# Causal attention on one core: every pair's first head keeps its probabilities whole in fp32, the second is always split

## The chip, the cores and the metric

One core of one Trainium2 chip runs the whole program. The metric is the device time of one execution in microseconds. Before the change it was run three times.

## The reference, cut to what matters

The input x is 4 images of 64 channels and 32 x 32 = 1024 places. Three layers follow each other; the one that the change touches most is the second.

```python
# layer 1, on x as (b, 64, 1024): media attention, one head, no mask
att = softmax(einsum('bmi,bmj->bij', k, q), axis=2)
x = x + einsum('cm,bmn->bcn', wo, einsum('bij,bmj->bmi', att, v))
# layer 2, on tokens t = (b, 1024, 64): causal attention, 8 heads of 64
q, k, v = (layernorm(t) @ W for W in (Wq, Wk, Wv))          # (b, 8, 1024, 64)
scores = where(causal, -1e30, einsum('bhqd,bhkd->bhqk', q, k) / 8)
t = t + (softmax(scores) @ v).reshape(b, 1024, 512) @ Wo
# layer 3: recurrence over the 1024 tokens, batch-normalised input
y[t] = sigmoid(wx[t] + y[t-1] @ V.T);  t = t + y
```

## The kernel before, in words

**Items.** The attention scores are made transposed, keys on the 128 partitions and 512 queries (four tiles of 128) along a PSUM bank. One such bank is an item. The first layer has 16 items in each of 4 units (one unit a batch), slots 0 to 63. The causal layer has 16 units, each two heads of one batch (a pair, `r` = 0 and 1), with 9 items a head: 36 tiles of the lower triangle, packed four to an item by `ATTN_RUNS`. Items of the two heads alternate, so item n of a unit belongs to head n % 2, and one slot of two items is worked at a time: `g`, `g+1`. There are 64 + 288 items.

**What happens to an item.** TensorE makes the scores of both heads in three fp16 products (keys high x queries high and low, keys low x queries high; `pe_scores`, L526, matmul at L537), after identity products that add the mask where a tile is on the diagonal (L522). ScalarE takes the exponential to fp32 (`act_item`, L775, to the tile `probs`) and, for a split item, once more to fp16 (L779, `probs_high`). GpSimd subtracts the second from the first into `probs_low` (`pool_low`, L1250). Three slots later (`LAG` = 6 items) TensorE multiplies by the values, the probabilities being the stationary side, a tile at a time (`pe_values`, L545): three fp16 products for a split item (L574 high x values high, L576 high x values low, L578 low x values high), or one fp32 product for a whole item (L570, `probs` x `values`). The column of ones behind the 64 values gives the denominator. VectorE divides (`dve_scale`, L975) and GpSimd adds the result to the tokens (L1260).

**Which items are whole.** `whole(i)` (L143) decides it for all engines: in the first layer every 4th item, in the causal layer the last of every 6, so n = 5, 11 and 17 of a unit of 18, all of head 1.

**Buffers and waits.** Scores have three banks (`ST_RING`): TensorE waits until ScalarE is through with the item two before (L517). `probs` and the fp16 parts are rings of ten items. Before ScalarE overwrites a place of `probs` it waits for GpSimd's low part of the item ten before, or, if that one was whole, for TensorE's values of it (L770 to L773). The third item of each head (`SPLIT_ITEM`) has half its tiles' values done a slot later (`value_runs`, L126).

**What lies beside it.** Each slot also makes, for the unit after the next, the products whose row maxima are subtracted (`pe_maxes`, L497, masks at L483), and VectorE reduces them (L903); they have two banks, each freed by VectorE. Auxiliary steps share one more bank: queries (two a unit), values (two a unit, four token tiles each for both heads), the maxima transposed (L614), keys (L651). The products of these steps go through `pe_split_product` (L455, L456). For values, ScalarE copies the bank to `values` in fp32 and to `values_high` in fp16 (L810, L811), and VectorE subtracts to `values_low` (L959). GpSimd also works on the layer norms of each batch (`pool_ln1`, `pool_newton`, L1269 to L1296) between its low parts.

The order on TensorE in a slot is: values of the items six before, auxiliary steps, masks of the maxima, masks of the scores, maxima, scores. Every engine runs its own list in this order of slots, without reordering. After the last item the third layer follows (from L698).

Of the kernel before, what the change touches and what calls it, by code (L numbers as in the profile page):

```python
# [26 lines left out]
ST_RING, P_RING, E_RING, Q_RING, S_RING = 3, 10, 10, 3, 4  # L27
LAG = 6

CONV_WHOLE, ATTN_WHOLE = 4, 6  # L30
LN_EPS = 1e-5


# [79 lines left out]
def unit_of(i):  # L113
    return i // CONV_ITEMS if i < CONV_ITEMS * B else B + (i - CONV_ITEMS * B) // (2 * ATTN_ITEMS)
# [28 lines left out]
def whole(i):  # L143

    n = i - first_slot(unit_of(i))
    period = CONV_WHOLE if unit_of(i) < B else ATTN_WHOLE
    return n % period == period - 1


def rests(i):  # L150
# [77 lines left out]
def build(nc, x_cm, x_tm, conv_w, conv_vo, attn_w, ffn, gb, const, out):  # L228
# [5 lines left out]
    with ctx:  # L234
# [37 lines left out]
        e32 = sb("probs", [P, E_RING, CW])  # L272
        p_hi = sb("probs_high", [P, P_RING, CW], f16)
        p_lo = sb("probs_low", [P, P_RING, CW], f16)
        v32 = [sb(f"values{i}", [P, NT, 2, PO]) for i in range(2)]
        v_hi = [sb(f"values_high{i}", [P, NT, 2, PO], f16) for i in range(2)]
        v_lo = [sb(f"values_low{i}", [P, NT, 2, C], f16) for i in range(2)]
        scaled = sb("scaled_outputs", [P, S_RING, TPC, C])
        rden = sb("reciprocal_denominators", [P, S_RING, TPC])
        cmx = [sb(f"conv_partial_max{i}", [P, NT, NC]) for i in range(2)]  # L280
# [264 lines left out]
        def pe_values(i):  # L545
            v = unit_of(i)
            n = i - first_slot(v)
            r = 0 if v < B else n % 2
            if n == 0:
                nc.tensor.wait_ge(s_aux_used, values_ready(v))  # L550
            if whole(i):
                nc.tensor.wait_ge(s_probs, i + 1)
            else:
                nc.tensor.wait_ge(s_rest, rests(i))
            for item, (j, t0, tiles, at) in value_runs(i):
                for k in range(tiles):
                    c, t = (t0 + k) // TPC, (t0 + k) % TPC
                    half = half_of(v, c, r)
                    opens = half not in OPENED
                    if opens:  # L560
                        OPENED.add(half)
                        if half == B * NC + 1:
                            pe_wait_bank(OUTPUT_BANK_HAD)
                        elif 1 <= half <= B * NC:
                            nc.tensor.wait_ge(s_scaled, half)
                        elif half:
                            nc.tensor.wait_ge(s_scaled, half - 1)
                    cols, dst = slice((at + k) * P, (at + k + 1) * P), output_bank(half)[:, t * PO:t * PO + PO]
                    if whole(item):
                        ins = nc.tensor.matmul(dst, e32[:, item % E_RING, cols], v32[v % 2][:, j, r, :],  # L570
                                               start=opens, stop=True, skip_group_check=True)
                        continue
                    hi, lo = p_hi[:, item % P_RING, cols], p_lo[:, item % P_RING, cols]
                    nc.tensor.matmul(dst, hi, v_hi[v % 2][:, j, r, :], start=opens, stop=False,  # L574
                                     skip_group_check=True)
                    nc.tensor.matmul(dst[:, 0:C], hi, v_lo[v % 2][:, j, r, :], start=False, stop=False,  # L576
                                     skip_group_check=True)
                    ins = nc.tensor.matmul(dst, lo, v_hi[v % 2][:, j, r, :], start=False, stop=True,  # L578
                                           skip_group_check=True)
            ins.then_inc(s_values, 1)  # L580

# [207 lines left out]
        def act_aux(m):  # L789
            _, _, what, k = AUXES[m]  # L790
            bank = aux_bank(m)
            if what in ("max_transpose", "max_transpose_half"):
                return
            nc.scalar.wait_ge(s_aux, m + 1)
            if what == "conv_matrix":
                nc.scalar.activation(wov_hi[:], bank[:, 0:C], ACT.Copy).then_inc(s_aux_cast, 1)
            elif what == "project":
                act_project(bank, k).then_inc(s_aux_cast, 1)
            elif what == "conv_values":

                if k >= 2:
                    nc.scalar.wait_ge(s_values, first_slot(k - 1))
                x = bank[:].rearrange("p (t c) -> p t c", c=C)
                nc.scalar.activation(v32[k % 2][:, :, 0, 0:C], x, ACT.Copy)
                nc.scalar.activation(v_hi[k % 2][:, :, 0, 0:C], x, ACT.Copy).then_inc(s_aux_cast, 1)
            elif what == "values":
                v, c = k // 2, k % 2
                nc.scalar.wait_ge(s_values, first_slot(v - 1))
                x, tiles = bank[:].rearrange("p (t r c) -> p t r c", r=2, c=C), slice(c * TPC, (c + 1) * TPC)
                nc.scalar.activation(v32[v % 2][:, tiles, :, 0:C], x, ACT.Copy)  # L810
                nc.scalar.activation(v_hi[v % 2][:, tiles, :, 0:C], x, ACT.Copy).then_inc(s_aux_cast, 1)  # L811
            elif what == "queries":
                nc.scalar.activation(q_hi[k // 2 % Q_RING][:, k % 2 * CW:(k % 2 + 1) * CW], bank[:],
                                     ACT.Copy).then_inc(s_aux_cast, 1)
            elif what == "matrix":
                nc.scalar.activation(of_heads(a_hi if k < 2 else pr_hi, k % 2), by_pair(bank),
                                     ACT.Copy).then_inc(s_aux_cast, 1)
            elif what == "keys":
                nc.scalar.activation(xs_hi[:, k * CW:(k + 1) * CW], bank[:], ACT.Copy).then_inc(s_aux_cast, 1)
            elif what == "ln3_transpose":  # L820
                nc.scalar.activation(xh3T[:, k * CW:(k + 1) * CW], bank[:], ACT.Copy).then_inc(s_aux_used, 1)
            else:
                nc.scalar.activation(wx_raw[:, k * CW:(k + 1) * CW], bank[:], ACT.Copy).then_inc(s_aux_used, 1)
# [117 lines left out]
        def dve_aux(m):  # L941
# [4 lines left out]
            if what == "conv_matrix":  # L946
                nc.vector.tensor_tensor(out=wov_lo[:], in0=bank[:, 0:C], in1=wov_hi[:],
                                        op=ALU.subtract).then_inc(s_aux_used, 1)
            elif what == "project":
                dve_project(bank, k).then_inc(s_aux_used, 1)  # L950
            elif what == "matrix":
                hi, lo = (of_heads(x, k % 2) for x in ((a_hi, a_lo) if k < 2 else (pr_hi, pr_lo)))
                nc.vector.tensor_tensor(out=lo, in0=by_pair(bank), in1=hi, op=ALU.subtract).then_inc(s_aux_used, 1)
            elif what == "conv_values":
                nc.vector.tensor_tensor(out=v_lo[k % 2][:, :, 0, :], in0=bank[:].rearrange("p (t c) -> p t c", c=C),
                                        in1=v_hi[k % 2][:, :, 0, 0:C], op=ALU.subtract).then_inc(s_aux_used, 1)
            elif what == "values":
                v, tiles = k // 2, slice(k % 2 * TPC, (k % 2 + 1) * TPC)
                nc.vector.tensor_tensor(out=v_lo[v % 2][:, tiles, :, :],  # L959
                                        in0=bank[:].rearrange("p (t r c) -> p t r c", r=2, c=C),  # L960
                                        in1=v_hi[v % 2][:, tiles, :, 0:C], op=ALU.subtract).then_inc(s_aux_used, 1)
            elif what == "queries":
                v, cols = k // 2, slice(k % 2 * CW, (k % 2 + 1) * CW)
                nc.vector.tensor_tensor(out=q_lo[v % Q_RING][:, cols], in0=bank[:], in1=q_hi[v % Q_RING][:, cols],
                                        op=ALU.subtract).then_inc(s_aux_used, 1)
            elif what == "keys":
                cols = slice(k * CW, (k + 1) * CW)
                nc.vector.tensor_tensor(out=xs_lo[:, cols], in0=bank[:], in1=xs_hi[:, cols],
                                        op=ALU.subtract).then_inc(s_aux_used, 1)
            elif what == "wx":  # L970
                nc.vector.wait_ge(s_aux_used, m + 1)
                for h in range(2):
                    nc.vector.bn_stats(bst[:, 2 * k + h, :], wx_raw[:, (2 * k + h) * HW:(2 * k + h + 1) * HW])
# [106 lines left out]
        def _(dve):  # L1080
# [10 lines left out]
                                        op=ALU.subtract).then_inc(s_x16, 1)  # L1091
            for i in range(2):
                nc.vector.memset(amx[i][:], -3e38)
                nc.vector.memset(v32[i][:, :, :, C:PO], 1.0)
                nc.vector.memset(v_hi[i][:, :, :, C:PO], 1.0)
                ins = nc.vector.memset(y16[i][:, :, 0:1], 0.0)
            ins.then_inc(s_init, 1)
            for k in range(3):
# [377 lines left out]
```

## Time and profile before

| what | us |
|---|---|
| median of three runs | 568.92 |
| lowest, highest run | 566.38, 571.42 |
| profiled execution (the page gives its span, and no time beside it) | 567.0 |
| TensorE matmuls busy in it | 490.0 (86%) |
| ScalarE / GpSimd / VectorE busy | 429.3 / 424.4 / 398.8 |
| causal items: first scores, last values | about 110.9, 519.6 |

How to read it: PE is TensorE's matmul side and PEld its weight loads, which run ahead of and under the matmuls; DVE is VectorE, ACT ScalarE, POOL GpSimd, SP SyncE. Times of rows are from the start of the span. Matmuls are pipelined, so that the duration of one (some 196 ns for 65 columns) is no measure of how many fit in a microsecond; the distance from one weight load to the next is.

### The profile page before, as it was taken

How to read it: one execution, taken by the hardware profiler on the slowest of the kernel's cores; microseconds unless marked ns; L12 is line 12 of the kernel's file. 1: busy time of each engine (PE TensorE's matmuls, PEld its weight loads, DVE VectorE, ACT ScalarE, POOL GpSimd, SP SyncE). 2: the span in 40 equal slices, each digit the busy share in tenths (PEclk: the TensorE clock that was granted, in tenths of full speed). 3: DMA queues.
4: the chain of work that ended last, by engine and by line, in shares of the span. 5: the costliest groups of instructions: out<-in, count | busy, mean ns of one | idle time of the engine just before them, and what ended most of it. 6: DMA issues, size and time to landing. Idle time of an engine off the chain costs nothing.

```text
span 567.0 us, 16744 instructions
## 1 busy us (share of the span) xinstructions
PE 490.0 (86%) x6771; PEld 323.0 (57%) x6771; DVE 398.8 (70%) x909; ACT 429.3 (76%) x832; POOL 424.4 (75%) x463
## 2 busy tenths in 40 slices
PE   4699978988799998889999988998999999787783
PEld 1277655655565755565666756565666766564431
DVE  5878888767678786576767676766767786328757
ACT  3488867866778878587888878787888878785593
POOL 3867965857988797968788797899788799985002
PEclk9999999989999999799999999999999999998698
DMA  9100000000000000000000000000000000000001
GB/s 230 68 3 2 2 20 1 4 1 3 1 22 2 3 3 2 3 1 21 2 3 2 4 3 1 21 3 1 1 3 3 2 3 2 2 2 2 0 2 74
DMA packets 3580, 7.46 MB, mean 13 GB/s; under 512 B 1168, under 2 KB 1456, under 8 KB 3376
## 3 DMA queue, kind: packets, MB, share of 16 engines
q1 hardware_dynamic: 3056, 5.34, 3.5%
q8 instruction: 54, 0.88, 0.7%
q10 hardware_dynamic: 448, 1.05, 0.6%
q14 instruction: 22, 0.18, 0.1%
HBM read 4.22 MB, written 1.05 MB: 9 GB/s over the span
## 4 chain that ended last, share of the span: by engine, by line
PE 45%; DVE 22%; POOL 17%; ACT 9%; issue 6%; DMA 1%; DVEq 0%; SPq 0%; POOLq 0%; ACTq 0%
POOL probs_low L1250 10%; PE bank L537 9%; DVE attn_partial_max L903 7%; ACT probs_high L779 6%; PE bank L497 6%; PE bank L570 5%; PE bank L574 4%; DVE conv_partial_max L897 3%; PE bank L578 3%; PE bank L576 3%; PE bank L455 2%; PE bank L522 2%; PE bank L483 2%; PE bank L456 2%; POOL tokens L1260 2%
## 5 line engine op out<-in xcount | busy, mean ns | idle before, releaser
L1250 POOL TENSOR_TENSOR probs_low<-probs,probs_high 128x512 f16<-128x512 f32 x288 | 327.6, 1158 | 77.5 <-ACT probs_high L779 76.7
L775 ACT ACTIVATE probs<-bank 128x512 f32<-128x512 f32 x352 | 214.7, 611 | 84.2 <-PE bank L537 69.0
L903 DVE TENSOR_REDUCE attn_partial_max<-bank 128x1 f32<-128x512 f32 (+2 forms) x288 | 185.3, 685 | 99.5 <-PE bank L497 99.0
L779 ACT ACTIVATE probs_high<-bank 128x512 f16<-128x512 f32 x288 | 176.8, 614 | 0.0
L574 PEld LDWEIGHTS bank<-values_high,probs_high 128*128 128x128 f16 x1152 | 105.7, 98 | 74.2 <-issue 35.8
L574 PE MATMUL bank<-values_high,probs_high 128*128 128x65 f16 x1152 | 128.8, 196 | 15.5 <-POOL probs_low L1250 11.4
L576 PE MATMUL bank<-values_low,probs_high 128*128 128x64 f16 x1152 | 127.6, 194 | 0.0
L578 PE MATMUL bank<-values_high,probs_low 128*128 128x65 f16 x1152 | 127.1, 194 | 0.0
L576 PEld LDWEIGHTS bank<-values_low,probs_high 128*128 128x128 f16 x1152 | 106.9, 99 | 3.2
L578 PEld LDWEIGHTS bank<-values_high,probs_low 128*128 128x128 f16 x1152 | 107.2, 98 | 0.0
L570 PE MATMUL bank<-values,probs 128*128 128x65 f32 x512 | 71.7, 278 | 0.8 <-POOL probs_low L1250 0.8
L570 PEld LDWEIGHTS bank<-values,probs 128*128 128x128 f32 x512 | 64.7, 192 | 3.5 <-POOL probs_low L1250 1.0
L497 PE MATMUL bank<-attn_keys_high,queries_high 64*128 64x512 f16 (+3 forms) x384 | 56.7, 332 | 7.9 <-ACT probs_high L779 6.0
L1260 POOL TENSOR_TENSOR tokens<-scaled_outputs,tokens 128x256 f32<-128x256 f32 x71 | 51.7, 729 | 8.0 <-DVE scaled_outputs L983 3.3
L537 PE MATMUL bank<-queries_high,attn_keys_high 64*128 64x512 f16 (+3 forms) x384 | 55.6, 326 | 1.1 <-ACT probs_high L779 1.1
L537 PE MATMUL bank<-queries_high,attn_keys_low 64*128 64x512 f16 (+3 forms) x384 | 55.5, 325 | 0.0
L537 PE MATMUL bank<-queries_low,attn_keys_high 64*128 64x512 f16 (+3 forms) x384 | 55.5, 325 | 0.0
L897 DVE TENSOR_REDUCE conv_partial_max<-bank 128x1 f32<-128x512 f32 x64 | 42.8, 687 | 5.8 <-PE bank L470 4.7
L983 DVE TENSOR_TENSOR scaled_outputs<-bank,reciprocal_denominators 128x256 f32<-128x256 f32 x72 | 30.6, 425 | 7.6 <-DVE reciprocal_denominators L979 0.5
L522 PE MATMUL bank<-causal_masks,identity_bf 128*128 128x128 bf16 x256 | 27.5, 219 | 6.6 <-ACT probs_high L779 6.4
L497 PEld LDWEIGHTS bank<-attn_keys_high,queries_high 64*128 64x128 f16 x384 | 15.3, 93 | 29.7 <-issue 6.8
L1343 POOL TENSOR_TENSOR x_split<-probs 128x512 f32<-128x512 f32 x4 | 4.2, 1092 | 36.1 <-ACT probs L878 36.1
(192 smaller groups left out, 708.9 us busy)
## 6 DMA issues: line engine op xcount, KB each, us to landing
x_channels<-in_x_cm SPq DMA_DIRECT2D x6, 256.0 KB, 7.6
tokens<-in_x_tm SPq DMA_DIRECT2D x1, 1024.0 KB, 10.4
out<-ln_channels SPq DMA_DIRECT2D x4, 256.0 KB, 2.0
attn_weights<-in_attn_w ACTq DMA_DIRECT2D x1, 512.0 KB, 6.2
attn_keys_split<-attn_keys_high SPq DMA_DIRECT2D x4, 128.0 KB, 2.3
attn_keys_split<-attn_keys_low SPq DMA_DIRECT2D x4, 128.0 KB, 2.4
queries_high<-minus_max_rows SPq DMA_DIRECT2D x32, 2.0 KB
x_channels<-in_x_cm ACTq DMA_DIRECT2D x2, 128.0 KB, 3.2
```

Source lines behind the costliest of these rows:

```text
L497: last[r] = nc.tensor.matmul(prep_bank(m + r)[:, at * P:(at + tiles) * P], q[rows(r), t * P:(t + 1) * P], xs_hi[rows(r), b * N + j0 * P:b ...
L537: last[r] = nc.tensor.matmul(ST[(i + r) % ST_RING][:, at * P:(at + tiles) * P], keys[rows(r), b * N + j * P:b * N + (j + 1) * P], queries[ ...
L570: ins = nc.tensor.matmul(dst, e32[:, item % E_RING, cols], v32[v % 2][:, j, r, :], start=opens, stop=True, skip_group_check=True)
L574: nc.tensor.matmul(dst, hi, v_hi[v % 2][:, j, r, :], start=opens, stop=False, skip_group_check=True)
L576: nc.tensor.matmul(dst[:, 0:C], hi, v_lo[v % 2][:, j, r, :], start=False, stop=False, skip_group_check=True)
L578: ins = nc.tensor.matmul(dst, lo, v_hi[v % 2][:, j, r, :], start=False, stop=True, skip_group_check=True)
L775: ins = nc.scalar.activation(e32[:, i % E_RING, :], o[:], ACT.Exp, scale=scale)
L779: ins = nc.scalar.activation(p_hi[:, i % P_RING, :], o[:], ACT.Exp, scale=scale)
L897: nc.vector.reduce_max(cmx[v % 2][:, t, part:part + 1], o[:], AX).then_inc(s_prep_used, 1)
L903: nc.vector.reduce_max(dst, o[:].rearrange("p (n w) -> p n w", n=n), AX).then_inc(s_prep_used, 1)
L1250: nc.gpsimd.tensor_tensor(out=p_lo[:, i % P_RING, :], in0=e32[:, i % E_RING, :], in1=p_hi[:, i % P_RING, :], op=ALU.subtract).then_inc(s_r ...
L1260: nc.gpsimd.tensor_tensor(out=dst, in0=scaled[:, half % S_RING, :, :], in1=dst, op=ALU.add).then_inc(s_added, 1)
```

## The change

In the causal layer every item of head 0 of a pair (n even) is whole and every item of head 1 is split. The values of head 0 are then kept only in fp32 and those of head 1 only as fp16 high and low parts, so that each of ScalarE's two copies and VectorE's subtraction handles one head. The first layer keeps its rule of every fourth item. Its values move to buffers without the head dimension.

```diff
-CONV_WHOLE, ATTN_WHOLE = 4, 6
+CONV_WHOLE = 4
+WHOLE_HEAD, SPLIT_HEAD = 0, 1
...
 def whole(i):
     n = i - first_slot(unit_of(i))
-    period = CONV_WHOLE if unit_of(i) < B else ATTN_WHOLE
-    return n % period == period - 1
+    return n % CONV_WHOLE == CONV_WHOLE - 1 if unit_of(i) < B else n % 2 == WHOLE_HEAD
...
-        v32 = [sb(f"values{i}", [P, NT, 2, PO]) for i in range(2)]
-        v_hi = [sb(f"values_high{i}", [P, NT, 2, PO], f16) for i in range(2)]
-        v_lo = [sb(f"values_low{i}", [P, NT, 2, C], f16) for i in range(2)]
+        v32 = [sb(f"values{i}", [P, NT, PO]) for i in range(2)]
+        v_hi = [sb(f"values_high{i}", [P, NT, PO], f16) for i in range(2)]
+        v_lo = [sb(f"values_low{i}", [P, NT, C], f16) for i in range(2)]
...
-                        ins = nc.tensor.matmul(dst, e32[:, item % E_RING, cols], v32[v % 2][:, j, r, :],
+                        ins = nc.tensor.matmul(dst, e32[:, item % E_RING, cols], v32[v % 2][:, j, :],
...
-                nc.scalar.activation(v32[v % 2][:, tiles, :, 0:C], x, ACT.Copy)
-                nc.scalar.activation(v_hi[v % 2][:, tiles, :, 0:C], x, ACT.Copy).then_inc(s_aux_cast, 1)
+                nc.scalar.activation(v32[v % 2][:, tiles, 0:C], x[:, :, WHOLE_HEAD, :], ACT.Copy)
+                nc.scalar.activation(v_hi[v % 2][:, tiles, 0:C], x[:, :, SPLIT_HEAD, :], ACT.Copy).then_inc(s_aux_cast, 1)
...
-                nc.vector.tensor_tensor(out=v_lo[v % 2][:, tiles, :, :],
-                                        in0=bank[:].rearrange("p (t r c) -> p t r c", r=2, c=C),
-                                        in1=v_hi[v % 2][:, tiles, :, 0:C], op=ALU.subtract).then_inc(s_aux_used, 1)
+                nc.vector.tensor_tensor(out=v_lo[v % 2][:, tiles, :],
+                                        in0=bank[:].rearrange("p (t r c) -> p t r c", r=2, c=C)[:, :, SPLIT_HEAD, :],
+                                        in1=v_hi[v % 2][:, tiles, 0:C], op=ALU.subtract).then_inc(s_aux_used, 1)
```

The remaining lines of the diff drop the head index from the other value products (L574 to L578), from the first layer's copies (L804, L805, L955) and from the two memsets that write the columns of ones (L1094, L1095).

## Rows read from the trace of the kernel before

**Rows 1.** The page, part 1: busy time, share of the span, instructions.
```profile
PE 490.0 (86%) x6771; PEld 323.0 (57%) x6771; DVE 398.8 (70%) x909; ACT 429.3 (76%) x832; POOL 424.4 (75%) x463
```

**Rows 2.** Who waited for whom: engine, line, waited for, us in total, times, longest.
```profile
ACT probs L775 <- PE bank L537: 69.0, 105, 4.1
...
PEld bank L574 <- POOL probs_low L1250: 33.4, 56, 3.6
...
PE bank L574 <- POOL probs_low L1250: 11.4, 17, 3.1
```

**Rows 3.** The page, part 5: costliest groups, busy us and mean ns, idle before.
```profile
L1250 POOL TENSOR_TENSOR probs_low<-probs,probs_high 128x512 f16<-128x512 f32 x288 | 327.6, 1158 | 77.5 <-ACT probs_high L779 76.7
...
L779 ACT ACTIVATE probs_high<-bank 128x512 f16<-128x512 f32 x288 | 176.8, 614 | 0.0
L574 PEld LDWEIGHTS bank<-values_high,probs_high 128*128 128x128 f16 x1152 | 105.7, 98 | 74.2 <-issue 35.8
...
L570 PEld LDWEIGHTS bank<-values,probs 128*128 128x128 f32 x512 | 64.7, 192 | 3.5 <-POOL probs_low L1250 1.0
```

**Rows 4.** Timeline of PEld, 302 to 327: start us, us, what, [idle before].
```profile
302.34 0.10 PEld L574 LDWEIGHTS bank<-values_high,probs_high 128*128 128x128 f16 x1 [0.21 <-issue]
...
304.64 0.10 PEld L574 LDWEIGHTS bank<-values_high,probs_high 128*128 128x128 f16 x1 [0.42 <-issue]
...
305.36 0.10 PEld L455 LDWEIGHTS bank<-attn_keys_split,qk_matrix_high 128*128 128x128 f16 x1
...
306.93 0.10 PEld L574 LDWEIGHTS bank<-values_high,probs_high 128*128 128x128 f16 x1 [0.42 <-issue]
...
309.29 0.10 PEld L574 LDWEIGHTS bank<-values_high,probs_high 128*128 128x128 f16 x1 [0.42 <-issue]
...
312.00 0.10 PEld L574 LDWEIGHTS bank<-values_high,probs_high 128*128 128x128 f16 x1 [0.42 <-issue]
...
314.44 0.10 PEld L574 LDWEIGHTS bank<-values_high,probs_high 128*128 128x128 f16 x1 [0.42 <-POOL probs_low L1250]
...
317.69 0.10 PEld L574 LDWEIGHTS bank<-values_high,probs_high 128*128 128x128 f16 x1 [0.21 <-issue]
...
320.20 0.10 PEld L574 LDWEIGHTS bank<-values_high,probs_high 128*128 128x128 f16 x1 [0.42 <-POOL probs_low L1250]
...
322.91 0.10 PEld L574 LDWEIGHTS bank<-values_high,probs_high 128*128 128x128 f16 x1 [0.21 <-issue]
...
326.04 0.10 PEld L574 LDWEIGHTS bank<-values_high,probs_high 128*128 128x128 f16 x1 [0.21 <-issue]
```

**Rows 5.** Timeline of PEld, the same unit: where it stood behind value products.
```profile
303.64 0.12 PEld L497 LDWEIGHTS bank<-attn_keys_high,queries_high 64*128 64x128 f16 x2 [0.52 <-DVE attn_partial_max L903]
...
307.78 0.13 PEld L483 LDWEIGHTS bank<-causal_masks,identity_bf 128*128 128x128 bf16 x2 [0.15 <-DVE attn_partial_max L903]
...
319.00 0.13 PEld L522 LDWEIGHTS bank<-causal_masks,identity_bf 128*128 128x128 bf16 x2 [0.52 <-DVE attn_partial_max L903]
```

**Rows 6.** Timeline of PEld, 111.9 to 113.2: a whole item, then a split one.
```profile
111.89 0.97 PEld L570 LDWEIGHTS bank<-values,probs 128*128 128x128 f32 x8 [0.42 <-issue]
112.72 0.15 PEld L574 LDWEIGHTS bank<-values_high,probs_high 128*128 128x128 f16 x1
...
113.17 0.10 PEld L455 LDWEIGHTS bank<-value_matrix_high,attn_keys_split 128*128 128x128 f16 x1
```

**Rows 7.** Timelines of POOL and PEld near 227; then engines' busy us, clock 228 to 230.
```profile
226.55 0.61 POOL L1291 COPY ln_out<-ln_out 128x512 f32<-128x512 f32 x1
...
228.33 0.10 PEld L574 LDWEIGHTS bank<-values_high,probs_high 128*128 128x128 f16 x1 [3.58 <-POOL probs_low L1250]
...
228.00:230.00 2.00, 1.39 (x23) 1.23 (x24) 0.00 (x0) 0.00 (x0) 2.00 (x3) 0.50 0.00 0
```

**Rows 8.** Timelines of POOL and DVE at the end of the causal layer.
```profile
511.37 6.73 POOL L1250 TENSOR_TENSOR probs_low<-probs,probs_high 128x512 f16<-128x512 f32 x6
...
520.17 0.17 DVE L979 RECIPROCAL reciprocal_denominators<-bank 128x4 f32<-128x4 f32 x1
```

More of the change, by code:

```diff
@@ L573, in pe_values @@
                     hi, lo = p_hi[:, item % P_RING, cols], p_lo[:, item % P_RING, cols]
-                    nc.tensor.matmul(dst, hi, v_hi[v % 2][:, j, r, :], start=opens, stop=False,
+                    nc.tensor.matmul(dst, hi, v_hi[v % 2][:, j, :], start=opens, stop=False,
                                      skip_group_check=True)
-                    nc.tensor.matmul(dst[:, 0:C], hi, v_lo[v % 2][:, j, r, :], start=False, stop=False,
+                    nc.tensor.matmul(dst[:, 0:C], hi, v_lo[v % 2][:, j, :], start=False, stop=False,
                                      skip_group_check=True)
-                    ins = nc.tensor.matmul(dst, lo, v_hi[v % 2][:, j, r, :], start=False, stop=True,
+                    ins = nc.tensor.matmul(dst, lo, v_hi[v % 2][:, j, :], start=False, stop=True,
                                            skip_group_check=True)
@@ L803, in act_aux @@
                 x = bank[:].rearrange("p (t c) -> p t c", c=C)
-                nc.scalar.activation(v32[k % 2][:, :, 0, 0:C], x, ACT.Copy)
-                nc.scalar.activation(v_hi[k % 2][:, :, 0, 0:C], x, ACT.Copy).then_inc(s_aux_cast, 1)
+                nc.scalar.activation(v32[k % 2][:, :, 0:C], x, ACT.Copy)
+                nc.scalar.activation(v_hi[k % 2][:, :, 0:C], x, ACT.Copy).then_inc(s_aux_cast, 1)
             elif what == "values":
@@ L954, in dve_aux @@
             elif what == "conv_values":
-                nc.vector.tensor_tensor(out=v_lo[k % 2][:, :, 0, :], in0=bank[:].rearrange("p (t c) -> p t c", c=C),
-                                        in1=v_hi[k % 2][:, :, 0, 0:C], op=ALU.subtract).then_inc(s_aux_used, 1)
+                nc.vector.tensor_tensor(out=v_lo[k % 2][:], in0=bank[:].rearrange("p (t c) -> p t c", c=C),
+                                        in1=v_hi[k % 2][:, :, 0:C], op=ALU.subtract).then_inc(s_aux_used, 1)
             elif what == "values":
                 v, tiles = k // 2, slice(k % 2 * TPC, (k % 2 + 1) * TPC)
-                nc.vector.tensor_tensor(out=v_lo[v % 2][:, tiles, :, :],
-                                        in0=bank[:].rearrange("p (t r c) -> p t r c", r=2, c=C),
-                                        in1=v_hi[v % 2][:, tiles, :, 0:C], op=ALU.subtract).then_inc(s_aux_used, 1)
+                nc.vector.tensor_tensor(out=v_lo[v % 2][:, tiles, :],
+                                        in0=bank[:].rearrange("p (t r c) -> p t r c", r=2, c=C)[:, :, SPLIT_HEAD, :],
+                                        in1=v_hi[v % 2][:, tiles, 0:C], op=ALU.subtract).then_inc(s_aux_used, 1)
             elif what == "queries":
@@ L1093, in _ @@
                 nc.vector.memset(amx[i][:], -3e38)
-                nc.vector.memset(v32[i][:, :, :, C:PO], 1.0)
-                nc.vector.memset(v_hi[i][:, :, :, C:PO], 1.0)
+                nc.vector.memset(v32[i][:, :, C:PO], 1.0)
+                nc.vector.memset(v_hi[i][:, :, C:PO], 1.0)
                 ins = nc.vector.memset(y16[i][:, :, 0:1], 0.0)
```

## The prediction, as it was made before the result

> **What bounds the kernel now.** I read the page first: in the span of 567.0 us TensorE's matmuls are busy 86%, its weight loads 57%, and ScalarE, GpSimd and VectorE 70 to 76% [rows 1]. No engine is full, so the waits come next: ScalarE waits 69.0 us for TensorE's scores, while TensorE's value products wait for GpSimd's low parts (11.4 us on the matmul side, 33.4 us as the weight loads see it) [rows 2]. Each engine waits for the next in a circle. The groups give the prices: a low part on GpSimd 1.16 us, an exponential on ScalarE 0.61 us, and a weight load of 98 ns in fp16 against 192 ns in fp32 [rows 3].
>
> Then the weight loads in order of time. One unit of attention (two heads) is nine slots, each with the values of one pair of items, the next maxima and the next scores. Slot starts k=0 to 8 lie at 302.34, 304.64, 306.93, 309.29, 312.00, 314.44, 317.69, 320.20 and 322.91, and the next unit at 326.04 [rows 4]: lengths 2.30, 2.29, 2.36, 2.71, 2.44, 3.25, 2.51, 2.71 and 3.13, together 23.70 us. A pair of split items takes 304.64 to 305.36, 0.72 us, though it is 24 matmuls [rows 4]. After such a pair TensorE often stands still: in k=0 it could go on at 303.06 (0.72 behind 302.34) and goes on at 303.64; k=6 likewise (318.41, 319.00) [rows 4, 5]. The row names VectorE's maxima, but what comes last there is ScalarE: both exponentials of the item two back must end before a score bank is free, the same 2.3 us in each such slot. So in regular slots two loops tie: ScalarE's (two exponentials of one item, then 1.0 us of maxima and scores on TensorE) and TensorE's own.
>
> **The change, part by part.** Per unit 9 of 18 items are whole where 3 were: 6 more in each of 16 units, 96 in all. The conv items stay as they are.
>
> GpSimd loses 96 x 1.16 = 111 us, ScalarE 96 x 0.61 = 59 us [rows 3]. Neither is a gain by itself: it is worth what TensorE now waits for them.
>
> TensorE pays. A whole item of 4 tiles followed by a split one stands at 111.89: fp32 loads start at 111.89, the fp16 ones at 112.72, and the next work at 113.17 [rows 6]. The pair costs 0.83 + 0.45 = 1.28 us, against 0.72 for two split items: 0.56 us more. In a unit, k = 0, 1, 4, 6, 7 go from split+split to whole+split (5 x 0.56); k = 2, 5, 8 hold one whole item already and only change the order; k = 3 (which takes two tiles over from k = 2) gets four more whole tiles for four split ones, 0.51. That is 3.31 us a unit, 53 us over 16 units. All of it is on TensorE.
>
> Here the Trainium skill can be weighed. It says that a true fp32 product goes through the array in four passes ("FP8 and Floating Point Precision", TensorE Precision Notes). The three fp16 products of a tile (0.72/8 = 0.09 us) would then become 0.12 us; the trace has 0.83/4 = 0.21, so it disagrees with passes alone, and by passes the whole change would add only 12 us. The skill also says that the fast weight load is off for fp32 ("TensorE: Matmul & The Clock Gate", Weight-path perf modes); the trace's 192 against 98 ns agrees, and this is the rule that speaks against the change.
>
> What comes back is TensorE's standing time. With the first item whole, its bank is free after one exponential: 0.61 us plus some 0.15 us of hand-over, covered by 1.28 us of value products. So the stalls go: 0.55 us at k=0, 0.05 at k=1, 0.46 at k=2 (it continues at 307.78 and waits again before the maxima), 0.14 at k=3, 0.58 at k=6, 0.11 at k=8 [rows 4, 5], 1.89 us a unit; each is the gap between what the slot's pieces take where nothing holds them and what they take here. The regular unit becomes 23.70 + 3.31 - 1.89 = 25.1 us, now TensorE from end to end. Is another engine late next? ScalarE needs at most 3 x 0.61 = 1.83 us a slot and GpSimd one low part of 1.16 us with a few additions of outputs a unit [rows 3]; the slots average 2.79 us. The tightest is k=2, with values of two tiles each: I put it at 1.90 us, so ScalarE just fits there. If it didn't fit I would lose at most the 0.46 us, 7 us over all units.
>
> Fourteen units have the maxima beside them: 14 x 1.89 = 26.5 us. In the last two GpSimd is behind the whole time (six low parts in a row from 511.37, and VectorE's closing scale only at 520.17 [rows 8]); slot by slot I count 5.0 and 5.1 us back, 10.1 together, 1.2 of it behind the last scores, where 3 x 1.28 us of products remain.
>
> The other stalls behind GpSimd come where it works on the layer norms. The largest: it is through with the norm at 226.55 + 0.61, and TensorE starts again at 228.33 after 3.58 us, at the lower of TensorE's two clocks (0.50 granted, 1.2 GHz) [rows 7]. GpSimd would come to that block about 0.6 us earlier and have one low part instead of two behind it, while TensorE comes later: about 1.3 us of it stays, too little standing for me to expect the lower clock again. Over the units I count 12 us back in such places (3.4 in the fourth unit, 2.7 in the ninth, 1.5 in the first and fifth, 1.3 in the eleventh, 1.6 in the rest); that this is near the 11.4 us of the wait row [rows 2] is a check on it. Bounds: 8 if the norms' stalls mostly stay, 16 if all go.
>
> The values: ScalarE's two copies and VectorE's subtraction go from 512 to 256 columns a half, 64 copies and 32 subtractions. No row has a 256-column copy; each saves between nothing and 0.61 us [rows 3], I take half. These engines aren't the bound, and the copies only feed values needed slots later: worth 0 here, 0 to 1 us. The smaller memsets at the start lie before the first scores: 0. The waits change form (a whole item's buffer is given back by TensorE's values and not by GpSimd), but those values are issued a full slot before ScalarE asks: 0. Queued behind that wait would be all later exponentials, so if it did bind, every slot would show it.
>
> **The sum.** +53.0 - 26.5 - 10.1 - 12.0 = +4.4 us on a span of 567.0. The page gives the profiled execution by its span alone; the median of the three runs is 568.92, 1.9 above it, with runs from 566.38 to 571.42. I add the change to the median: 573.3 us, in round numbers 573 us, +0.7%. A measurement of this kernel tells about 1% from no change, 5.7 us.
>
> **Rivals.**
> *The stalls stay (slower).* VectorE's name stands on the regular stalls. If its two maxima of a slot, or k=2 and its neighbours, hold TensorE up still, half of the 26.5 us doesn't come back: +4.4 + 13 = +17, near 586; with a third, 582. For it: the release row names it [rows 5]. Against: the slots get longer and VectorE gets no more to do.
>
> *The whole item is cheap in its new place (faster).* Each whole item now follows the scores, where weight loads idle for 0.42 us [rows 4]. If its first fp32 load slips under that, a pair costs less than 1.28 us. The result turns from slower to faster at 1.28 - 4.4/96 = 1.23 us a pair, and beats 1% at 1.175 us; with 0.2 us hidden in each of 96 places it is 573 - 19 = 554 us. Against: the one pair that stands so, at 111.89, has the same 0.42 us in front of it and still costs 1.28 [rows 6]. Most of this rival's 0.09 is for part of that saving. The four-pass rule of the Trainium skill would be its far end (12 us added where I have 53, so 532 us), and by the 0.21 us a tile of [rows 6] I give that end 0.01 of the 0.09.
>
> *Nothing moves.* If the true floor is all stalls gone (I count 52 us of them, 3 more than I take back), the change is +1 us: 570. That the switch of heads doesn't act as said (288 low parts would remain) I hold for excluded by the code: one function decides it for all engines.
>
> **How the numbers follow.** Forecast 0.65, of which 0.46 lies within 1% of 568.92 and 0.19 above (its own range 569 to 578: the 8 to 16 us of the norms, 0.46 us at k=2). Stalls stay: 0.20, all slower. Cheap whole item: 0.09, of which 0.07 is faster by over 1%. Nothing moves: 0.06, within 1%. Faster 0.07, within 1% 0.54, slower 0.39. The range takes most of the slower rival and the near end of the other: 565 to 582.
>
> **What would show it.** In the changed profile the fp32 value products should be 512 + 768 = 1280 records and low parts 192. A regular unit should last 25.1 us, with the pair's values 1.28 us in nearly every slot, TensorE over 90% busy, and the waits of value products on GpSimd down from 11.4 to under 3 us. ScalarE and GpSimd should wait for TensorE far more than now. Wrong would be: a pair at under 1.2 or over 1.35 us; a regular unit at 24 or at 26.5 us; a half-clock stretch near 227 us that remains; stalls of 0.5 us left at k=0 and k=6.

## The result, and the profile after

The changed kernel takes 577.54 us (median of four runs, 575.63 to 582.26), the kernel before 568.83 (four runs, 566.38 to 571.42): a ratio of 1.0156, 95% interval 1.0116 to 1.0196. On a second chip it was 1.0169 (1.0135 to 1.0202). The change makes the kernel 1.6% slower. The profiled execution after took 576.86 us with a span of 575.0, 8.0 above the span of before.

The page after, part 1, to be read beside [rows 1], and four of its groups, beside [rows 3]:

```profile
PE 528.0 (92%) x6387; PEld 372.1 (65%) x6387; DVE 390.7 (68%) x909; ACT 377.1 (66%) x736; POOL 318.7 (55%) x367
...
L1250 POOL TENSOR_TENSOR probs_low<-probs,probs_high 128x512 f16<-128x512 f32 x192 | 221.2, 1157 | 191.9 <-ACT probs_high L779 191.2
L775 ACT ACTIVATE probs<-bank 128x512 f32<-128x512 f32 x352 | 195.5, 599 | 133.4 <-PE bank L537 120.1
...
L570 PEld LDWEIGHTS bank<-values,probs 128*128 128x128 f32 x1280 | 156.3, 191 | 56.6 <-issue 46.6
```

ScalarE lost 52 us of busy time, GpSimd 106 and TensorE gained 38. The low parts went from 288 to 192 and the fp32 loads from 512 to 1280. The two engines that were relieved now stand idle in front of TensorE: GpSimd's low parts waited 77.5 us for their input before and 191.9 now. The waits tell the same (engine and line, waited for, total us, times, longest), beside [rows 2]:

```profile
ACT probs L775 <- PE bank L537: 120.1, 143, 4.6
...
PEld bank L570 <- ACT probs_high L779: 7.1, 14, 0.9
...
PEld bank L574 <- POOL probs_low L1250: 4.1, 9, 1.0
...
PE bank L574 <- POOL probs_low L1250: 2.0, 3, 0.9
```

ScalarE's wait for scores rose from 69.0 to 120.1 us, and TensorE's wait for low parts fell from 11.4 to 2.0 us.

A regular unit after, the timeline of weight loads, beside [rows 4]. Each slot now starts with the fp32 loads of a whole item:

```profile
306.92 0.97 PEld L570 LDWEIGHTS bank<-values,probs 128*128 128x128 f32 x8 [0.21 <-issue]
...
309.29 0.97 PEld L570 LDWEIGHTS bank<-values,probs 128*128 128x128 f32 x8 [0.42 <-issue]
310.12 0.15 PEld L574 LDWEIGHTS bank<-values_high,probs_high 128*128 128x128 f16 x1
...
310.56 0.10 PEld L455 LDWEIGHTS bank<-attn_keys_split,qk_matrix_high 128*128 128x128 f16 x1
...
312.08 0.52 PEld L570 LDWEIGHTS bank<-values,probs 128*128 128x128 f32 x4 [0.42 <-issue]
...
314.16 1.41 PEld L570 LDWEIGHTS bank<-values,probs 128*128 128x128 f32 x12 [0.44 <-ACT probs_high L779]
...
317.27 0.97 PEld L570 LDWEIGHTS bank<-values,probs 128*128 128x128 f32 x8 [0.42 <-issue]
...
320.09 0.97 PEld L570 LDWEIGHTS bank<-values,probs 128*128 128x128 f32 x8 [0.42 <-issue]
...
323.36 0.97 PEld L570 LDWEIGHTS bank<-values,probs 128*128 128x128 f32 x8 [0.21 <-issue]
...
325.84 0.97 PEld L570 LDWEIGHTS bank<-values,probs 128*128 128x128 f32 x8 [0.42 <-issue]
...
329.11 0.97 PEld L570 LDWEIGHTS bank<-values,probs 128*128 128x128 f32 x8 [0.21 <-issue]
...
332.14 0.97 PEld L570 LDWEIGHTS bank<-values,probs 128*128 128x128 f32 x8 [0.21 <-issue]
```

The reader is to see two things. The whole and split pair is 309.29 to 310.12 to 310.56: 0.83 + 0.44 = 1.27 us. And the unit runs from 306.92 to 332.14, 25.22 us, against 23.70. The distances between such rows, k=0 to 8, are the measure for all that follows. "Unit" is the same regular unit in each run:

| kernel | k0 | k1 | k2 | k3 | k4 | k5 | k6 | k7 | k8 | unit |
|---|---|---|---|---|---|---|---|---|---|---|
| before | 2.30 | 2.29 | 2.36 | 2.71 | 2.44 | 3.25 | 2.51 | 2.71 | 3.13 | 23.70 |
| after | 2.37 | 2.79 | 2.08 | 3.11 | 2.82 | 3.27 | 2.48 | 3.27 | 3.03 | 25.22 |
| e1, both heads' values | 2.37 | 2.80 | 2.08 | 3.11 | 2.82 | 3.27 | 2.48 | 3.28 | 3.13 | 25.34 |
| e2, head 1 whole | 2.36 | 2.79 | 2.22 | 3.09 | 2.81 | 3.25 | 2.51 | 3.26 | 3.13 | 25.42 |
| e3, price only | 2.37 | 2.80 | 2.21 | 3.11 | 2.82 | 3.27 | 2.51 | 3.26 | 3.03 | 25.38 |
| e4, gain only | 1.81 | 2.24 | 2.08 | 3.01 | 2.29 | 2.71 | 2.01 | 2.70 | 2.86 | 21.71 |
| e5, pairs 2 5 8 | 1.82 | 2.30 | 2.35 | 2.79 | 2.41 | 3.27 | 2.02 | 2.71 | 3.13 | 22.80 |
| e6, pairs 2 3 8 | 1.82 | 2.23 | 2.22 | 3.11 | 2.43 | 2.70 | 2.25 | 2.71 | 3.13 | 22.60 |
| e7, pairs 2 3 6 8 | 1.81 | 2.24 | 2.21 | 3.11 | 2.29 | 2.71 | 2.48 | 2.71 | 3.13 | 22.69 |
| e8, pairs 2 8 | 1.81 | 2.29 | 2.36 | 2.72 | 2.43 | 2.70 | 2.26 | 2.71 | 3.13 | 22.41 |

Where the 8.0 us of span lie: the values behind the first causal scores (still a first-layer pair, items 59 and 60; the first causal values come two slots later) began at 112.74 instead of 111.89, which is 0.85 us from stages that both kernels have alike; from there to the third layer's first weight load, which follows the last value products, it is 415.52 against 408.48 us, 7.04 more; behind that 46.74 against 46.63. One trace is not exact to the microsecond in these parts. In the thirteen traces of this case the first mark lies anywhere between 111.89 and 115.95 us, and the kernel before has the earliest. The second trace of the changed kernel (e11) takes 413.96 us between the two marks, 5.5 more than before, and 1.5 of the difference to the first trace lies in the first causal unit.

The norm block of the fourth and fifth unit, beside [rows 7]: in the timelines GpSimd's last operation of the norm and TensorE's next split item:

```profile
230.94 0.61 POOL L1291 COPY ln_out<-ln_out 128x512 f32<-128x512 f32 x1
...
232.72 0.10 PEld L574 LDWEIGHTS bank<-values_high,probs_high 128*128 128x128 f16 x1 [1.02 <-POOL probs_low L1250]
```

and the windows row there (length, busy us of PE, PEld, DVE, ACT and POOL, granted clock, DMA):

```profile
232.00:234.00 2.00, 1.28 (x18) 0.69 (x20) 0.00 (x0) 0.68 (x2) 1.86 (x3) 1.00 0.00 0
```

The stall is 1.02 us in place of 3.58, and the clock is granted in full (2.4 GHz) where it was at 1.2 before.

### The profile page after: what moved, and what is told of

Same layout as the page of the kernel before. It is cut to its first block, busy times and chain, and to the rows that moved or that the text cites. A ratio compares the mean times of both kernels' runs of the same rounds, so it can differ in the third digit from the quotient of the medians.

```text
span 575.0 us, 15784 instructions
## 1 busy us (share of the span) xinstructions
PE 528.0 (92%) x6387; PEld 372.1 (65%) x6387; DVE 390.7 (68%) x909; ACT 377.1 (66%) x736; POOL 318.7 (55%) x367
## 4 chain that ended last, share of the span: by engine, by line
PE 72%; DVE 14%; POOL 7%; issue 3%; ACT 2%; DMA 1%; SPq 0%; DVEq 0%; POOLq 0%; ACTq 0%
PE bank L570 24%; PE bank L537 14%; PE bank L497 7%; POOL probs_low L1250 3%; DVE conv_partial_max L897 3%; PE bank L574 3%; DVE attn_partial_max L903 3%; PE bank L578 3%; PE bank L576 3%; PE bank L455 3%; PE bank L456 3%; PE bank L483 2%; PE bank L522 2%; PE bank L470 1%; DVE queries_low L964 1%
## 5 line engine op out<-in xcount | busy, mean ns | idle before, releaser
L1250 POOL TENSOR_TENSOR probs_low<-probs,probs_high 128x512 f16<-128x512 f32 x192 | 221.2, 1157 | 191.9 <-ACT probs_high L779 191.2
L775 ACT ACTIVATE probs<-bank 128x512 f32<-128x512 f32 x352 | 195.5, 599 | 133.4 <-PE bank L537 120.1
L570 PEld LDWEIGHTS bank<-values,probs 128*128 128x128 f32 x1280 | 156.3, 191 | 56.6 <-issue 46.6
L570 PE MATMUL bank<-values,probs 128*128 128x65 f32 x1280 | 175.5, 280 | 3.4 <-DVE scaled_outputs L983 3.4
L779 ACT ACTIVATE probs_high<-bank 128x512 f16<-128x512 f32 x192 | 116.3, 606 | 0.0
L574 PE MATMUL bank<-values_high,probs_high 128*128 128x65 f16 x768 | 89.1, 195 | 2.2 <-POOL probs_low L1250 2.0
L576 PE MATMUL bank<-values_low,probs_high 128*128 128x64 f16 x768 | 89.0, 193 | 0.0
L578 PE MATMUL bank<-values_high,probs_low 128*128 128x65 f16 x768 | 88.8, 194 | 0.0
L574 PEld LDWEIGHTS bank<-values_high,probs_high 128*128 128x128 f16 x768 | 79.7, 108 | 8.6 <-POOL probs_low L1250 4.1
L576 PEld LDWEIGHTS bank<-values_low,probs_high 128*128 128x128 f16 x768 | 71.1, 99 | 3.2
L578 PEld LDWEIGHTS bank<-values_high,probs_low 128*128 128x128 f16 x768 | 71.2, 98 | 0.0
## 6 DMA issues: line engine op xcount, KB each, us to landing
tokens<-in_x_tm SPq DMA_DIRECT2D x1, 1024.0 KB, 11.4
```

What stands on the lines that cost most here:

```text
L574: nc.tensor.matmul(dst, hi, v_hi[v % 2][:, j, :], start=opens, stop=False, skip_group_check=True)
L576: nc.tensor.matmul(dst[:, 0:C], hi, v_lo[v % 2][:, j, :], start=False, stop=False, skip_group_check=True)
L578: ins = nc.tensor.matmul(dst, lo, v_hi[v % 2][:, j, :], start=False, stop=True, skip_group_check=True)
L775: ins = nc.scalar.activation(e32[:, i % E_RING, :], o[:], ACT.Exp, scale=scale)
L779: ins = nc.scalar.activation(p_hi[:, i % P_RING, :], o[:], ACT.Exp, scale=scale)
L1250: nc.gpsimd.tensor_tensor(out=p_lo[:, i % P_RING, :], in0=e32[:, i % E_RING, :], in1=p_hi[:, i % P_RING, :], op=ALU.subtract).then_inc(s_r ...
```

## The experiments

The first four ran on one chip (before: 570.06 us, nine runs), e5 to e8 on one (569.01, seven runs), e9 to e11 on one (569.52, eleven runs).

**e1: the same whole items, both heads' values copied in both forms.** The edit is to the kernel before:

```diff
-    period = CONV_WHOLE if unit_of(i) < B else ATTN_WHOLE
-    return n % period == period - 1
+    if unit_of(i) < B:
+        return n % CONV_WHOLE == CONV_WHOLE - 1
+    return n % 2 == 0
```

> The changed kernel's choice of whole items (every item of head 0) in the buffers of the kernel before: ScalarE copies both heads to fp32 and to fp16 as before, 512 columns a copy, and VectorE subtracts both. Theory (TensorE's fp32 products are the price, nothing else is near the bound): 577.5 us, the same as the changed kernel within 2 us. Rival (the halved copies are on the path): 64 copies and 32 subtractions at half price are worth up to 64 x 0.24 + 32 x 0.3 = 25 us, so this kernel would take some 590 to 600 us.

581.01 us (five runs), ratio 1.0189 (1.0167 to 1.0212), where the change has 1.0156 and 1.0169. The intervals overlap, so the times alone can't part them; the slots can: all are equal but k=8, which is 3.13 us where the change has 3.03. The halved copies and subtraction are worth 0.1 us in the regular unit and some 2 us in all, not 25.

**e2: head 1 whole and head 0 split**, `return n % 2 == 1` in e1's edit.

> As e1, but head 1 of every pair is whole and head 0 split. The same number of fp32 products, the other order in a slot: ScalarE must make both exponentials of the first item before its score bank is free. Theory: in most slots TensorE's values (1.28 us) cover these 1.1 to 1.25 us; at k=2, with 0.65 us of values, 0.4 to 0.5 us a unit of standing comes back, so 577.5 + 7 = 584 us. If the order is worth nothing: 577.5 us. If ScalarE's hand-over was what the change gained by: over 595 us.

580.81 us, 1.0187 (1.0159 to 1.0215), the same as e1. The stall came back at k=2 as expected, but with 0.14 us, not 0.4 to 0.5. The timeline of weight loads in that slot:

```profile
315.57 0.13 PEld L484 LDWEIGHTS bank<-causal_masks,identity_bf 128*128 128x128 bf16 x2 [0.17 <-DVE attn_partial_max L904]
315.95 0.10 PEld L498 LDWEIGHTS bank<-attn_keys_high,queries_high 64*128 64x128 f16 x2 [0.25 <-ACT probs_high L780]
```

VectorE's maxima hold the masks here as in the changed kernel (below), and only what the second row adds is ScalarE's. At k=0 and k=6, where ScalarE now again makes both exponentials of the first item, nothing came back (2.36 and 2.51 us against 2.37 and 2.48): the longer value products cover its hand-over. With every second item whole, the order of the heads is worth almost nothing.

**e3: TensorE's price without the others' savings.** The edit to the changed kernel:

```diff
-            elif i >= E_RING:
+            if i >= E_RING:
                 nc.scalar.wait_ge(s_rest, rests(i - E_RING))
...
-            if not whole(i):
+            if not whole(i) or unit_of(i) >= B:
...
-                    if not whole(i):
+                    if not whole(i) or unit_of(i) >= B:
                         pool_low(i)
```

and `rests` counts the same items.

> The changed kernel, but ScalarE also makes the fp16 exponential and GpSimd the low part of every causal item; those of the whole items are not used. TensorE does what it does in the changed kernel, the other two engines get all 96 items' work back and 48 more. Theory (TensorE alone sets the pace): 577.5 us plus what GpSimd's layer norm blocks cost when it has 18 low parts a unit again, 0 to 10 us, so 578 to 588 us. Rival (the saving on ScalarE and GpSimd is what pays back the fp32 products): 577.5 + 46 = 620 us or more.

596.55 us, 1.0469 (1.0404 to 1.0534), 18 us above the change. Both numbers were off: it lies between the two. The slots part it: the regular unit is 25.38 us against 25.22, although GpSimd makes 18 low parts in it where the change makes 9. So there the saving on the two engines is worth 0.16 us. From the first causal values' slot to the third layer's first load the traces differ by 20.1 us (429.5 against 409.4): 9.4 in the second, fifth, ninth and eleventh units, which have slots behind norm blocks, 9.8 in the last two units and the tail, where GpSimd works almost without a pause, and 0.9 elsewhere. At the largest norm block, the timelines of POOL and PEld in e3:

```profile
235.79 0.61 POOL L1291 COPY ln_out<-ln_out 128x512 f32<-128x512 f32 x1
236.36 2.26 POOL L1250 TENSOR_TENSOR probs_low<-probs,probs_high 128x512 f16<-128x512 f32 x2
...
238.67 0.10 PEld L574 LDWEIGHTS bank<-values_high,probs_high 128*128 128x128 f16 x1 [2.76 <-POOL probs_low L1250]
```

and the row of its waits, 2.0 in the changed kernel:

```profile
PE bank L574 <- POOL probs_low L1250: 11.9, 12, 2.6
```

Two low parts follow the norm, TensorE waits for the second, and its slot there is 7.03 us (3.86 in the changed kernel). Behind that stall the granted clock was 0.50 (239 to 241 us).

**e4: the savings without TensorE's price.**

```diff
-                    if whole(item):
+                    if whole(item) and unit_of(item) < B:
```

> The changed kernel, but the values of whole causal items are multiplied as three fp16 products from old contents of the fp16 buffers in place of the fp32 product: this leaves the right values of head 0 out, so that only its time counts. ScalarE and GpSimd work as in the changed kernel. Theory: every one of 144 whole items costs TensorE 0.56 us less, 80 us in all, if nothing else binds: a regular unit of 25.2 - 5.0 = 20.2 us, 497 us in all; VectorE's two maxima need some 1.75 us a slot, so up to 505 us. Rival (the regular stalls are VectorE's, as their row says, and stay): a unit of 22 us and 525 us. If fp32 were not the price: over 550 us.

534.43 us, 0.9381 (0.9353 to 0.9409): 43 us below the change, where I expected 72 to 80. That fp32 is the price stands, but a regular unit is 21.71 us and not 20.2, because the next limits are close. The timeline of weight loads shows which, at k=2 and k=3:

```profile
294.56 0.13 PEld L483 LDWEIGHTS bank<-causal_masks,identity_bf 128*128 128x128 bf16 x2 [0.45 <-DVE attn_partial_max L903]
...
297.59 0.13 PEld L483 LDWEIGHTS bank<-causal_masks,identity_bf 128*128 128x128 bf16 x2 [0.58 <-DVE attn_partial_max L903]
```

Here VectorE's name is right: behind two fp16 pairs the masks wait for the maxima. At k=0 and k=6, where the same name stood before, the stalls are gone (1.81 and 2.01 us). And with TensorE faster, it runs into the norm blocks again (the slot is 6.33 us).

**e5: as many whole items as before and of the same pairs, but of head 0**, `return n in {4, 10, 16}`.

> The kernel before with three whole items a unit as it has, of the same pairs (k = 2, 5, 8), but of head 0 in place of head 1. TensorE's work and the counts of all engines stay. Theory (before the change the regular stalls are ScalarE's hand-over: it makes both exponentials of the first item before a score bank is free; a whole first item takes one of them away two slots ahead of its values): k=0 loses 0.45 us (2.30 to some 1.85), k=6 0.45 us (2.50 to 2.05), k=3 a little: 1.0 us a unit, 14 us over 14 units, so 556 us where before is 570. Rival (the stalls are VectorE's, as the row names it, or only the number of whole items matters): 570 us.

564.14 us, 0.9903 (0.9883 to 0.9923). The slots are as forecast: k=0 from 2.30 to 1.82, k=6 from 2.51 to 2.02, the unit 22.80. TensorE's work did not change, so these stalls were ScalarE's hand-over, not VectorE's. The total was forecast at 556: of the 0.9 us a unit, more than half was given back at the norms. The last slot of the first unit and the one after it take 5.72 + 4.59 us where before they took 4.78 + 3.00. GpSimd's norm block there is as long as before, the idle time of the weight loads in front of it 2.80 us instead of 1.86, and the granted clock behind it was 0.50, where before it stayed at 1.00.

**e6: pairs 2, 3 and 8 of head 0**, `return n in {4, 6, 16}`.

> As e5, but the whole items are those of pairs 2, 3 and 8 of head 0. The runs so far show k=2 and k=3 together at 5.07 us in the kernel before and 5.10 without any fp32 product, so something other than TensorE holds them, and a whole item of pair 3 should be nearly free, where one of pair 5 costs 0.56 us. Theory: a regular unit of some 22.1 us (before 23.70), 548 us in all. Rival (a whole item costs 0.56 us wherever it is): the same as e5, 556 us.

564.49 us, 0.9926 (0.9904 to 0.9948), the same as e5. Taking the whole item out of pair 5 brings k=5 from 3.27 to 2.70, the 0.56 us again. But pair 3 isn't nearly free: k=2 and k=3 together are 5.33 against 5.14 us, and k=6 loses 0.23. The two almost cancel.

**e7: a fourth, of pair 6**, `return n in {4, 6, 12, 16}`.

> As e6 with a fourth whole item, of pair 6. Theory: k=6 goes from 2.02 to 2.48 us, the regular unit to 22.6 us, and GpSimd's lighter load gives back some 3 us at the layer norms: 552 us. If GpSimd's load is what limits e6: 545 us or less.

562.10 us, 0.9891 (0.9840 to 0.9942). The regular unit is 22.69, as forecast; the interval holds e6 too.

**e8: pairs 2 and 8 only**, `return n in {4, 16}`.

> As e6 with only pairs 2 and 8 of head 0 whole, 2 whole items a unit. By TensorE alone a regular unit is some 22.0 us; GpSimd has 16 low parts and 4 additions, 16 x 1.14 + 2.9 = 21.1 us, 96% of it, so it should fall behind wherever it also works on a norm. Theory: the regular units as in e6, the units with norms longer: 550 to 558 us. If fewer whole items are always better: 545 us.

563.05 us, 0.9907 (0.9881 to 0.9933). The regular unit is the shortest of all, 22.41 us, and the time is not: TensorE's wait for low parts is 15.8 us here, against 9.6 in e7. What is saved in products is lost to GpSimd.

The regular units of e5 to e8 came within 0.5 us of their forecasts, the totals did not: they are 5 to 16 us above the 556, 548, 552 and 550 to 558 us expected. I had let nearly all of the gain in the regular units through to the total, and the norm blocks and the last units took back more than half of it.

**e9 and e10: the wait behind the norms attacked where it is.** To e7's rule come both items of single pairs, `or i in {82, 83, 138, 139, 218, 219, 326, 327}` (e10: the first four only).

> e7's whole items (pairs 2, 3, 6 and 8 of head 0) and, in four places, both items of the pair whose low parts GpSimd would make right behind a layer norm block: items 82, 83, 138, 139, 218, 219, 326 and 327. In e7 the slots there take 5.50 and 4.10, 5.43 and 4.55, 3.26 and 3.46, 3.13 and 3.02 us where their like take 3.13 and 2.9, 1.8 and 3.0, 2.3 and 2.7. Theory (these stalls are GpSimd's, and a whole item needs no GpSimd): each place pays up to 1.1 us of fp32 products and gets its stall back, 8 us in all, so 554 us where before is 569. Rival (the stall only moves to the next pair, whose low part waits as well): 560 to 562 us, as e7.

> As e9 with only the first two places (items 82, 83, 138 and 139), those with the long blocks of 6.6 us. Theory: they hold 7 of the 8 us, so 555 us; if the other two are worth as much: 558 us.

e9: 554.01 us (five runs), 0.9718 (0.9697 to 0.9738), the forecast. e10: 557.06, 0.9782 (0.9757 to 0.9808), so the first two places hold about five of the eight microseconds; in the traces the causal stretch goes from 392.6 (e7) to 387.3 (e10) and 384.4 us (e9). The slots at the first place go from 5.50 + 4.10 to 3.13 + 3.34. For the second, the windows of e7 (these kernels have one line more, so L574 is L575 there):

```profile
226.00:228.00 2.00, 0.00 (x0) 0.00 (x0) 0.00 (x0) 0.22 (x1) 1.88 (x4) 0.73 0.00 0
228.00:230.00 2.00, 1.57 (x25) 1.41 (x26) 0.00 (x0) 0.00 (x0) 1.90 (x3) 0.50 0.00 0
```

and its wait for low parts:

```profile
PE bank L575 <- POOL probs_low L1251: 9.6, 12, 3.5
```

The same windows of e9:

```profile
226.00:228.00 2.00, 2.00 (x16) 0.92 (x16) 0.81 (x2) 0.83 (x3) 1.73 (x5) 1.00 0.00 0
228.00:230.00 2.00, 0.80 (x12) 0.56 (x12) 1.60 (x5) 1.91 (x4) 2.00 (x3) 1.00 0.00 0
```

and its wait:

```profile
PE bank L575 <- POOL probs_low L1251: 3.9, 7, 1.2
```

In e7 TensorE does nothing for 2 us and then runs at half clock; in e9 it has two whole items to work on while GpSimd is on the norm. e9 beats the kernel before by 2.8% and the change by 4.3%.

**e11: the change again.**

> The changed kernel once more, on this chip beside e9 and e10, to have its ratio from more rounds and to compare it with e1, which copies both heads' values. Theory: ratio to before 1.016, so e1's 1.0189 is 0 to 3 us above it; if the halved copies are worth nothing, 1.019.

579.07 us (six runs), 1.0169 (1.0135 to 1.0202). Its regular unit is that of the first trace to 0.01 us a slot (25.22 the unit), so e1's 0.1 us at k=8 is real. The first causal unit is not: two of its slots take 4.99 + 2.80 us here and 6.19 + 3.14 in the first trace, for a reason that no run shows.

## Why the prediction was right or wrong

The forecast was 573 us and the change 577.5: inside the range, in the direction of the sum, and twice its size between the medians (+8.7 for a forecast of +4.4; +7.0 and +5.5 in the stretch it concerns, in the two traces of the changed kernel). The likeliest class was "within 1%" with 0.54; the measured +1.6% lies in the class with 0.39. The steps:

**The price of a pair** (1.28 us, from one place in the old trace, which was a pair of the first layer) was 1.27. With it the +53 us stands: 3.31 us a unit more on TensorE. The rival with a cheap whole item fell with this row, and the four-pass estimate with it: 0.83 us for four tiles is 0.21 us a tile in every unit.

**Where another engine sets the pace.** "TensorE from end to end" was right but for k=2. ScalarE and GpSimd aren't it: e3 gives both all their work back, and the regular unit moves by 0.16 us. e4 shows the counter-proof: without the fp32 price all these slots shrink, k=3 by only 0.10 us, because VectorE's maxima come next there.

**The stalls regained**, 48.6 us in the forecast, were 53.0 - 7.0 = 46.0 in the first trace (47.5 in e11's). This is the term that was mis-sized, in two parts:

- The regular ones: 26.5 forecast, about 25 measured (14 units of 23.70 + 3.31 - 25.22 = 1.79 us). The step that failed is k=2, "I put it at 1.90 us, so ScalarE just fits there". It is 2.08 us, and not ScalarE but VectorE's maxima are late. The timelines after, of DVE and of PE:

```profile
311.54 1.29 DVE L903 TENSOR_REDUCE attn_partial_max<-bank 128x1 f32<-128x512 f32 x2 [1.51 <-PE bank L497]
```

```profile
312.98 0.27 PE L483 MATMUL bank<-causal_masks,identity_bf 128*128 128x128 bf16 x2
```

  VectorE ends the maxima of k=1 at 312.83, and the masks of k=2, which need their banks, follow at 312.98; the value products before them had been issued by 312.8. I had counted k=0 at 2.31 (2.37), k=3 at 3.08 (3.11) and k=4 at 3.00 (2.82), so the errors mostly cancel: that the regular term came out near its forecast is in part luck.
- The norms: 12 forecast, 10.8 left by the difference (46.0 - 25.0 - 10.2), and 12.3 in e11's trace, so this term is not known to better than 1.5 us. The big one was right: its stall of 1.3 us is 1.02, and the half clock is gone.

**The last two units**, 10.1 us, gave 10.2: they and the tail behind the last slot's start went from 24.09, 13.44 and 5.42 us to 22.26, 13.26 and 3.84, with 6.6 us of products more.

**The values**, priced at 0 with an end at 1 us, are worth 0.1 us a unit, some 2 us (e1). The stall of 0.11 us at k=8, which I had put down to the pair's order, was theirs.

**The rest** of the difference between +4.4 and the 8.7 us of the medians is 0.85 us ahead of that stretch, 0.1 behind it and about 0.7 us by which medians and spans differ; nothing in the change explains these. With e11's trace the unexplained part is larger: 9.6 us between the medians there, 5.5 in the stretch that the change touches.

**What the stalls were.** I had read VectorE's name on the regular stalls as ScalarE's hand-over. e5 confirms it: with TensorE's and all engines' counts the same, a whole first item takes 0.48 us from k=0 and 0.49 from k=6. This is also what the change missed: three whole items in the right head give this relief, and it took nine.

**What brought the stalls back.** I had put it on the first item's bank, free after one exponential. In e2 and e3 ScalarE makes both exponentials of every first item, and k=0 and k=6 are as short as in the changed kernel to 0.03 us; in e3 1.63 of the 1.79 us of a regular unit come back (23.70 + 3.31 - 25.38). So it is the longer products that cover the hand-over, the other half of my sentence. On the whole kernel, beside 570.06 us before on the same chip, the price with no saving on the other engines adds 26.5 us, though its products are 53 us longer (e3, which even makes 48 low parts more than the kernel before). The savings on top of it are worth about 18 us, and without the price they are worth 35.6 (e4).

**What a whole item costs.** Across the table it is 0.56 us in a slot that TensorE fills (k = 0, 1, 5, 7 from e4 to the changed kernel), 0.4 to 0.5 at k = 4, 0.1 to 0.5 at k = 3 and k = 6, and nothing to 0.2 at k = 2 and k = 8.

Open: whether fewer low parts or earlier norms would lift e9 further wasn't tried, nor were e9's placement and the change's half copies put together.

## What to carry to other kernels

Work moved off two engines onto a third is worth only what the third was waiting for them: here 158 us less busy time on ScalarE and GpSimd cost 53 us of products, over half of the 46 us of stalls would have been filled by the longer products alone, and the lighter engines brought only the remaining 18 to 20. List the period's slots by length, name for each what comes last there, and put the more costly form only where the slot has a stall to fill or a hand-over to shorten; three well-placed items beat nine. And here a long block on a helper engine was bridged better by giving its customers a few items that don't need it (eight, 8 us) than by taking a third of the helper's low parts away everywhere.

## What the runs showed that I had not expected

**Small VectorE steps stretch under a low part.** At the end of the causal layer, the timelines of POOL and DVE of the changed kernel:

```profile
521.52 1.16 POOL L1250 TENSOR_TENSOR probs_low<-probs,probs_high 128x512 f16<-128x512 f32 x1 [0.47 <-ACT probs_high L779]
```

```profile
521.43 0.17 DVE L994 TENSOR_TENSOR ln_newton_scratch<-ln_rstd,ln_var_eps 128x4 f32<-128x4 f32 x1
521.63 1.07 DVE L995 SCALAR_TENSOR_TENSOR ln_newton_scratch<-ln_newton_scratch,ln_rstd 128x4 f32<-128x4 f32 x1
522.74 0.17 DVE L996 SCALAR_TENSOR_TENSOR ln_rstd<-ln_newton_scratch,ln_rstd 128x4 f32<-128x4 f32 x1
```

Four elements take 0.17 us, or 1.07 us when GpSimd's low part is under way: it ends at 522.68 and the VectorE step at 522.70. Before the change five such steps in a row took 5.5 us, the chain kept VectorE until about 520.2, and its closing scale began at 520.17 [rows 8], behind value products that were through at 519.6. The Trainium skill says that a VectorE operation with two SBUF inputs and a GpSimd operation that reads SBUF exclude each other for a whole instruction ("SBUF — State Buffer", SBUF: two separate sides); the trace agrees for L995, which ends 0.02 us behind the low part. The maxima, which VectorE reads from PSUM, keep their 0.69 us in all runs.

**The clock turns a stall into a longer one.** After 3.5 us without a product (e7, 224.6 to 228.2) the granted clock was 0.50 (1.2 GHz), and so it was after 2.6 us without a product in e3 (behind 238.7); after the 1.02 us of the changed kernel and at the same place in e9 it stayed at 1.00 (2.4 GHz). Part of what e9 gains should lie there; how much was not measured.
